# Rows of the 1/sigma ring widened from 9 to 16 floats in a fused LayerNorm, retention and FP4 feed-forward kernel

## What is computed

```
xn   = layernorm(x)                                  # each row: (x - mean) / sqrt(var + 1e-5)
Q, K = xpos(xn W_Q), xpos(xn W_K, downscale)         # 8 heads of 32
V    = xn W_V
S    = (Q K^T) * gamma^(n-m), causal                 # no softmax
Yn   = groupnorm_per_head(S V) * gn_weight + gn_bias
attn = (silu(xn W_G) * Yn) W_O
h    = silu(fp4(xn) fp4(w_gate)^T) * (fp4(xn) fp4(w_up)^T)   # 704 wide
out  = x + attn + fp4(h) fp4(w_down)^T
```

## Time and profile before

| | |
|---|---|
| median of 3 runs | 910.05 us (909.77 to 910.67) |
| the profiled execution, its own time | 908.67 us |
| its span, first to last instruction | 906.9 us |
| outside the span | 1.8 us |
| mean granted TensorE clock | 0.994 of full speed |
| busy: TensorE, VectorE, GpSimd, ScalarE | 96%, 92%, 74%, 54% |

### The profile page before, as it was taken

One profiled execution on the slowest core, in us unless ns is written; L12 is line 12 of the kernel. 1 busy time (PEld: TensorE's weight loads), 2 busy tenths in 40 slices (PEclk: granted clock), 3 DMA queues, 4 the chain that ended last, 5 costly groups with the idle time before them and its releaser, 6 DMA issues.

```text
span 906.9 us, 20369 instructions
## 1 busy us (share of the span) xinstructions
PE 870.9 (96%) x7698; PEld 762.5 (84%) x7698; DVE 834.6 (92%) x1883; ACT 493.7 (54%) x1358; POOL 673.4 (74%) x791
## 2 busy tenths in 40 slices
PE   1879999999999999999999999999999999999996
PEld 1668888888888888888888888888888888888885
DVE  7879999999999999999999999999999999999984
ACT  4555555555555555555555555555555555555552
POOL 5467777777778777777877777787777778777773
PEclk9999999999999999999999999999999999999998
DMA  9200110110111011011101101110110110110000
GB/s 339 69 1 19 36 37 18 37 37 19 36 36 36 19 37 35 19 36 36 31 24 36 37 18 37 35 32 23 36 33 22 37 37 26 29 37 12 8 13 18
DMA packets 30049, 33.62 MB, mean 37 GB/s; under 512 B 3328, under 2 KB 28672, under 8 KB 29696
## 3 DMA queue, kind: packets, MB, share of 16 engines
q1 hardware_dynamic: 29808, 32.26, 11.3%
q10 hardware_dynamic: 144, 0.07, 0.0%
HBM read 23.92 MB, written 8.39 MB: 36 GB/s over the span
## 4 chain that ended last, share of the span: by engine, by line
PE 94%; DVE 2%; POOL 1%; ACT 1%; DMA 1%; issue 0%; SPq 0%; POOLq 0%
PE quad L882 12%; PE quad L880 12%; PE quad L881 12%; PE quad L1057 5%; PE quad L941 4%; PE quad L964 4%; PE bank L880 3%; PE bank L881 3%; PE bank L882 3%; PE bank L996 3%; PE quad L1064 3%; PE quad L908 3%; PE quad L1041 2%; PE quad L965 2%; PE quad L929 2%; PE quad L933 2%
## 5 line engine op out<-in xcount | busy, mean ns | idle before, releaser
L880 PE MATMUL quad<-w_gu_hi,xqT_hi 128*128 128x512 f32 (+1 forms) x384 | 149.9, 390 | 3.0 <-DVE xqT_lo L586 3.0
L882 PE MATMUL quad<-w_gu_hi,xqT_lo 128*128 128x512 f32 (+1 forms) x384 | 145.2, 378 | 0.0
L881 PE MATMUL quad<-w_gu_lo,xqT_hi 128*128 128x512 f32 (+1 forms) x384 | 144.4, 376 | 0.0
L461 POOL TENSOR_TENSOR rstd<-var_eps,power 128x9 f32<-128x9 f32 x67 | 124.6, 1860 | 5.6
L452 POOL TENSOR_TENSOR x_quot<-xn,x_inv 128x256 f32<-128x256 f32 x64 | 41.0, 640 | 90.3 <-DVE x_inv L630 90.2
L469 POOL TENSOR_TENSOR xT_lo<-xT_in,xT_hi 128x256 fp32r<-128x256 f32 x64 | 47.0, 734 | 64.8 <-ACT xT_hi L775 64.8
L438 POOL TENSOR_TENSOR h_quot<-h,h_inv 128x704 f32<-128x704 f32 x64 | 88.9, 1389 | 6.3 <-DVE h_inv L577 1.3
L714 ACT ACTIVATE xqT_hi<-bank 128x256 fp32r<-128x256 f32 x64 | 24.5, 383 | 120.6 <-PE bank L916 120.6
L448 POOL TENSOR_TENSOR qk<-qk_cos,qk_sin 128x512 f32<-128x512 f32 x64 | 82.9, 1296 | 9.1 <-DVE qk_cos L589 1.4
L485 POOL TENSOR_TENSOR gate_gn<-gate,gn 128x512 f32<-128x512 f32 x64 | 82.7, 1292 | 0.2 <-ACT gate L768 0.2
L880 PEld LDWEIGHTS quad<-w_gu_hi,xqT_hi 128*128 128x128 f32 x384 | 72.6, 189 | 11.7 <-issue 3.2
(11 more groups left out here) (176 smaller groups left out, 2943.4 us busy)
## 6 DMA issues: line engine op xcount, KB each, us to landing
x_in<-in_x_dram SPq DMA_DIRECT2D x64, 128.0 KB, 2.2
xT_in<-in_xT_dram SPq DMA_DIRECT2D x64, 128.0 KB, 2.2
out_dram<-y_out SPq DMA_DIRECT2D x64, 128.0 KB, 1.7
sin<-const_sin_dram SPq DMA_DIRECT2D x1, 1792.0 KB, 10.9
raw<-in_w_gu_dram SPq DMA_DIRECT2D x2, 512.0 KB, 6.6
w_qkvg<-in_w_qkvg_dram SPq DMA_DIRECT2D x1, 1024.0 KB, 7.2
cos<-const_cos_dram SPq DMA_DIRECT2D x1, 896.0 KB, 7.0
raw<-in_w_down_dram SPq DMA_DIRECT2D x2, 352.0 KB, 7.3
```

The costliest lines, as they stand in the source:

```text
L461: pool.tensor_tensor(rstd[:, (t + 3) % RING, :], var_eps[:], power[:], ALU.pow).then_inc(rstd_ready, 1)
L880: pe.matmul(out, hi[:, k], w_hi[:, k], start=start, stop=False)
L881: pe.matmul(out, hi[:, k], w_lo[:, k], start=False, stop=False)
L882: return pe.matmul(out, lo[:, k], w_hi[:, k], start=False, stop=stop)
```

## The change

The ring's rows become 16 floats long; the same nine are written and the same eight read. No instruction is added, removed or moved.

```diff
-        rstd = sb("rstd", [P, RING, 1 + H])
+        rstd = sb("rstd", [P, RING, 16])
...
-                    pool.tensor_tensor(rstd[:, (t + 3) % RING, :], var_eps[:], power[:], ALU.pow).then_inc(rstd_ready, 1)
+                    pool.tensor_tensor(rstd[:, (t + 3) % RING, 0:1 + H], var_eps[:], power[:], ALU.pow).then_inc(rstd_ready, 1)
...
-                    pool.tensor_tensor(heads(y_gain[:]), heads(gate_gn[:, t % 2, 0, :]), spread(rstd[:, (t + 3) % RING, 1:], HD), ALU.mult).then_inc(gain_ready, 1)
+                    pool.tensor_tensor(heads(y_gain[:]), heads(gate_gn[:, t % 2, 0, :]), spread(rstd[:, (t + 3) % RING, 1:1 + H], HD), ALU.mult).then_inc(gain_ready, 1)
```

## The result

The changed kernel takes 905.60 us, the median of 6 runs (905.07 to 906.40), against 909.91 for the kernel before beside it (908.68 to 910.67): a ratio of 0.9952, 95% interval 0.9941 to 0.9963. It is faster by 4.3 us, outside the range of 907.8 to 912.2. The profiled execution took 905.44 us with a span of 903.6; the instructions are the same 20369.

The account below looks back on a forecast made before the run. The prediction took TensorE, busy throughout each 13.30 us step, as the bound. Its terms summed to 0 on TensorE and 0 within 0.2 us outside it, so the median forecast was 910.05 + 0, rounded to 910.0 us, range 907.8 to 912.2.

Parts of the forecast that it names:

- The bound: Steady step: TensorE busy for all 13.30 us, so every nanosecond on it counts; the other three engines have slack.
- TensorE, 512 columns: Matmuls of 512 columns, 232 ns apart: alignment term 0, although no row had an aligned stationary at a steady spacing.
- the two sizes above: TensorE matmuls of 128 and 256 columns, compared on and off multiples of 64: term 0 for each.
- the one size at which a dearer load of weights would show: TensorE's 128-column transposes, 109 ns each: load and stream are equally long in columns; term 0.
- The comparison behind it: TensorE rows with starts on multiples of 64 against rows 32 past: 112 ns both at 128 columns, term 0.
- A shift of their addresses against TensorE's can't free it: 512-column spacing: 232 ns also with ScalarE and GpSimd doing nothing, so other engines' accesses don't make it.
- Rival A: TensorE: aligned stationaries free the unnamed part of the spacing, up to 0.79 us a step, about 882 us; chance 0.09.
- the unnamed 19 ns in the 232: 512-column matmuls: spacing of 232 ns against 213 by column count at 2.4 GHz, with 19 ns unexplained by the profile.
- Rival B: TensorE's float32r matmuls: equal starts of stationaries and weights collide, 2 ns each, 0.11 us a step, 917 us; chance 0.09.
- VectorE, GpSimd, ScalarE: Work beside TensorE: term 0 each, hidden by slack or waiting; VectorE between -0.2 and +0.2 us.
- The unknown: Timeline rounding on 53 float32r matmuls a step, 0.5 ns each: 1.7 us, with VectorE's 0.2 giving +-1.9 about 910.

Follow-up runs that it names:

- xchain32: Kernel before, with only xn to xq moved onto multiples of 64 and buffers from xT_in on moved by 256 bytes: 910.04 us, ratio 1.0003.
- xT_only: Kernel before, with only the stationaries xT_hi, xT_lo, xqT_hi, xqT_lo at the changed kernel's place modulo 256: 905.16 us, ratio 0.9956.
- front32: Kernel before, with an unused 32-byte buffer ahead of all others, moving weights and activations together: 910.20 us, ratio 0.9998.
- ring16_gap32: Changed kernel, with an unused 32-byte buffer behind the ring, so buffers behind lie 256 bytes from their old place: 910.19 us, ratio 1.0009 to the kernel before.
- gap224: Kernel before, old ring kept, with an unused 224-byte buffer behind it giving the changed kernel's addresses: 905.51 us, ratio 0.9958.

## Why the prediction was wrong

*The bound* was read rightly: TensorE without a gap, 13.30 us a step, every nanosecond on it in the time. 61 steps x 67 ns (a little less where the state product is left out) are the 3.9 us found between the scores.

*The step that failed* is the term "TensorE, 512 columns": the prediction had no row with an aligned stationary at a steady spacing, and took 0 "by the two sizes above". Measured, the 24 products of 512 columns take 75 ns a step less and the 6 of 384 columns, which had no term of their own, 10 less: 85 together. The sizes it was carried over from did nothing (transposes of 128 columns) or went the other way (256 columns, 15 ns a step dearer); the other matmuls are 3 ns dearer, all of it on the first state products (line 908). The sum is the 67 ns of the step. The size of 128 columns was called "the one size at which a dearer load of weights would show", and it is the one at which nothing showed. A shape without a row of its own should have been bounded, not filled in from others.

*The comparison behind it* was also the wrong one. I set rows with starts on multiples of 64 against rows without, and the start is not what counts. Lines 908 and 1114, equal at 112 ns, did differ in the distance between their two operands (0 and 192 modulo 256), but at 128 columns distance seems to cost nothing: the transposes stayed at 109 ns in every run. Equal rows there said nothing of the longer streams. Line 1135 stood second in a short group behind a matmul of another kind, while the change's 227 ns come only after some ten products of 512 columns in a row.

*"A shift of their addresses against TensorE's can't free it"* held: xchain32 and xT_only show that the other engines' buffers have no part. The row it was drawn from could not show that, since VectorE was busy for 1.13 of its 1.16 us. But from it I went on to the weights, which "don't move", as if that settled TensorE's own side. That the weights stay is what changes the distance.

*Rival A* named the right part of the step, the unnamed 19 ns in the 232, and TensorE's loads as the taker, which fits but is not shown; but it tied the gain to starts 32 past a multiple of 64, and that was wrong. I gave it 0.09. It asked for up to 0.79 us a step and got 0.067 with the change, 0.14 with the best distance; even there the 512-column products stay at 226 to 237 ns, above the 213 of the columns. The Trainium skill's page "TensorE: Matmul & The Clock Gate" (Wait — 56ns, not 53.3ns?) has 215.7 ns at 512 columns. No run here reaches that, the shortest steady spacing being 224 ns; for this mix of float32r loads and streams the measurement decides against it. *Rival B*, that equal starts collide, names the distance 0 as the slow one. In sum the change came out faster and not slower. Its 2 ns on each 256-column matmul are nearly what the long run showed (118 to 120), though xT_only shows that most of this did not come from those products' own distance; its 512-column part is reversed.

*VectorE, GpSimd, ScalarE*: 0, as forecast: lines 652 and 438 are unchanged at 903 and 1389 ns, and line 461 takes 1.83 us, although each of its writes now crosses a multiple of 64. *The unknown* of 0.5 ns a matmul was reckoned from the timeline's rounding only, as if the cause itself could bring nothing. The real mean change on the 53 was 70 / 53 = 1.3 ns, against the 0.5 allowed.

What stays open is the mechanism. The runs show that the spacing follows the distance between TensorE's two operands modulo 256, repeatably, and that it depends on what streamed before. That the load and the stream disturb each other in SBUF is the reading that fits, and it is argued, not shown by itself. Why 192 is best and 160 worst was not tried; it would need a stream of loads and matmuls alone.

## What to carry to other kernels

Where TensorE streams without a gap, the placement of its stationary buffers against its streamed ones is a term of its own, here 1.3% of a step and 1.0% of the time between the worst and the best of eight distances. Sweep it with an unused buffer in steps of 32 bytes up to 256, and leave the sweep to the end, since every buffer added ahead shifts it; an edit that changes a buffer's size can move the time by 0.5% without doing anything. Judge such an edit against one that only restores the old addresses.

## What the runs showed of the hardware

Within a row of products of one size, at a granted clock of 1.00, the spacing of float32r matmuls of 512 columns lay between 224 and 238 ns and of 256 columns between 112 and 125 ns; it changed with the distance modulo 256 between the loaded and the streamed operand and with the products ahead. Moving every buffer together (front32), or one side by 256 (ring16_gap32, xchain32), leaves the step at 13300 ns to the nanosecond. Two runs with the same addresses (after and gap224) have the same 13233. The 128-column transposes stayed at 109 ns at each distance.

At half the clock nothing of this is left. Among the last 256-column products of the changed kernel, and in the window around them (columns as in the earlier trace rows), the granted clock is 0.50:

```profile
896.63 0.41 PE L965 MATMUL quad<-w_dn_lo,hT_hi 128*128 128x256 f32 x1
...
898.55 0.63 PE L1035 MATMUL quad<-w_dn_hi,hT_lo 128*128 128x256 f32 x2
```

```profile
896.60:898.60 2.00, 2.00 (x11) 2.00 (x11) 1.51 (x4) 0.24 (x1) 0.00 (x0) 0.50 0.00 0
```

Nine spacings take 1.92 us, 213 ns each, which is 256 columns at 1.2 GHz. In the kernel before, at distance 32, six take 1.28 us (901.11 to 902.39), again 213 each. So what a product takes beyond its columns, about 11 ns at 256 columns, and what the distance does to it, appear in these traces only at the full clock.
